# Where SyncE asks for the up weights, and where the flag's squares and product stand, in a two-layer gated network on one core

## The reference

```python
x = x + tanh(g_xattn[0]) * L0_xattn(ctx, layernorm(x))   # two graph attention layers, 8 heads of 32
x = x + tanh(g_ffn[0])   * L0_ffn(layernorm(x))          # silu(x gate^T * gs) * (x up^T * us), then down; inner 704
x = x + tanh(g_xattn[1]) * L1_xattn(ctx, layernorm(x))   # similarity of ctx, the top 76 of a row kept by sigmoid
x = x + tanh(g_ffn[1])   * L1_ffn(layernorm(x))          # 8 experts of width 512, the two best of a router
```

## Time and profile before

| | |
|---|---|
| median of 3 runs | 219.71 us (219.53 to 221.17) |
| the profiled execution's own time | 219.28 us |
| its span, first to last instruction | 217.3 us |
| outside the span | 1.98 us |
| granted TensorE clock over the span | 0.991 |
| PE busy | 201.7 us, 93% |
| DVE busy | 134.1 us, 62% |
| ACT and POOL busy | 85.8 and 85.9 us |

### The profile page before, as it was taken

One profiled execution on the slowest core, in us unless ns is written; L12 is line 12 of the kernel. 1 busy time (PEld: TensorE's weight loads), 2 busy tenths in 40 slices (PEclk: granted clock), 3 DMA queues, 4 the chain that ended last, 5 costly groups with the idle time before them and its releaser, 6 DMA issues.

```text
span 217.3 us, 3823 instructions
## 1 busy us (share of the span) xinstructions
PE 201.7 (93%) x1282; PEld 158.3 (73%) x1282; DVE 134.1 (62%) x461; ACT 85.8 (39%) x188; POOL 85.9 (40%) x107
## 2 busy tenths in 40 slices
PE   8999989999999999998989999999999999999930
PEld 7787764435885446788979998999973589999920
DVE  3696997999979969997788395853317601111200
ACT  2778653998001555034352263222225322222100
POOL 8256218420011020054640343543877656443222
PEclk9999999999999999999999999999999999999996
DMA  5768327139999115617142222322332310022322
GB/s 157 201 235 258 82 76 230 48 109 402 417 420 382 54 64 201 275 50 237 43 156 84 27 26 24 51 40 44 66 72 26 74 10 7 9 24 29 42 24 24
DMA packets 16797, 26.07 MB, mean 120 GB/s; under 512 B 4096, under 2 KB 12423, under 8 KB 16776
## 3 DMA queue, kind: packets, MB, share of 16 engines
q1 hardware_dynamic: 11328, 20.14, 25.8%
q0 software_dynamic: 4064, 5.25, 13.7%
q10 hardware_dynamic: 1382, 0.41, 1.1%
HBM read 21.34 MB, written 5.51 MB: 124 GB/s over the span
## 4 chain that ended last, share of the span: by engine, by line
PE 34%; DVE 32%; DMA 13%; issue 9%; ACT 7%; POOL 2%; DVEq 1%; POOLq 0%; ACTq 0%
PE PS L2081 13%; DMA out_dram<-a,ids_late 9%; PE PS L2113 6%; DMA out_dram<-zb,sidx 4%; PE PS L1784 3%; PE PS L2124 3%; DVE stat L1070 3%; DVE hT L1462 3%; ACT a L841 2%; PE PS L1848 2%; DVE work L1148 2%; DVE x L1322 1%; DVE mv L1077 1%; DVE work L1134 1%; DVE top L1144 1%
## 5 line engine op out<-in xcount | busy, mean ns | idle before, releaser
L2081 PE MATMUL PS<-hT,e 128*128 128x128 f32 x512 | 62.0, 276 | 1.1 <-ACT hT L970 1.1
L2081 PEld LDWEIGHTS PS<-hT,e 128*128 128x128 f32 x512 | 60.1, 192 | 2.9 <-ACT hT L970 1.9
L1966 PE MATMUL PS<-xnT,e 128*128 128x512 f32 x88 | 39.6, 598 | 2.0 <-DVE hT L1462 1.1
L1966 PEld LDWEIGHTS PS<-xnT,e 128*128 128x128 f32 x88 | 16.1, 190 | 22.2 <-issue 17.4
L1718 DVE TENSOR_TENSOR hT<-th,PS 128x512 f32<-128x512 f32 x15 | 10.3, 687 | 35.3 <-PE PS L2081 35.1
L2113 PE MATMUL PS<-e,hT 128*128 128x256 f32 x128 | 30.6, 382 | 0.2 <-DVE x L1500 0.2
L2113 PEld LDWEIGHTS PS<-e,hT 128*128 128x128 f32 x128 | 23.1, 190 | 2.8 <-issue 0.3
L646 POOL TENSOR_TENSOR rstd<-veps,nhalf 128x2 f32<-128x2 f32 x12 | 8.7, 728 | 39.4 <-DVE veps L1079 39.3
L709 POOL DMA_INDIRECT out_dram<-a,ids_early x8 | 13.0, 1629 | 24.1 <-ACT a L1004 11.4
L1980 PE MATMUL PS<-e,hT 128*128 128x256 f32 x96 | 21.7, 383 | 0.0
L1980 PEld LDWEIGHTS PS<-e,hT 128*128 128x128 f32 x96 | 17.9, 190 | 2.9 <-issue 0.5
(11 more groups left out here) (301 smaller groups left out, 316.5 us busy)
## 6 DMA issues: line engine op xcount, KB each, us to landing
e<-e_in SPq DMA_DIRECT2D x24, 512.0 KB, 8.6
x<-x_in SPq DMA_DIRECT2D x2, 512.0 KB, 6.3
graph_rows<-e SPq DMA_DIRECT2D x4, 256.0 KB, 2.1
out_dram<-x SPq DMA_DIRECT2D x4, 256.0 KB, 2.5
xn_rows<-xn SPq DMA_DIRECT2D x4, 256.0 KB, 2.4
e<-gw_in SPq DMA_DIRECT2D x1, 768.0 KB
e<-uw_in SPq DMA_DIRECT2D x1, 640.0 KB
e<-dw_in SPq DMA_DIRECT2D x1, 640.0 KB
```

The lines of the kernel that those rows point to most:

```text
L1966: mm = pe.matmul(PS[:, bank, :], w[:, k, it * P:(it + 1) * P], xnT[:, h, k, :], start=(k == 0), stop=(k == 1))
L2081: mm = pe.matmul(PS[:, bank + q, f * P:(f + 1) * P], w[:, k * F + f * P:k * F + (f + 1) * P], xgT[x_at][:, k, :], start=(k == 0), stop=(k ...
```

## The change

Three edits. SP waits for `row_picked[1]`, the gathered rows of tile 1, before it asks for `uw`, `gs`, `us`, `b1` and `ctxT`. On PE the flag's product goes ahead of `queries`. On ACT the second half of `sum_x` goes ahead of `weights`. No instruction is added or taken away besides SP's wait; line numbers behind it grow by one.

```diff
         PE_ORDER = [...
-                    ... ("weights", 0), ("feat", 1, 0), ("queries", 0), ("flag", 0),
+                    ... ("weights", 0), ("feat", 1, 0), ("flag", 0), ("queries", 0),
                     ("feat", 1, 1), ("sims", 0), ("sims", 1), ("graph_check", 0), ...
         ACT_ORDER = [...
-                     ("mix", 0), ("choice", 0), ("sum_hidden", 0), ("weights", 0), ("sum_x", 1), ("sum_hidden", 1),
+                     ("mix", 0), ("choice", 0), ("sum_hidden", 0), ("sum_x", 1), ("weights", 0), ("sum_hidden", 1),
                      ("feat", 1, 0), ("queries", 0), ("feat", 1, 1), ...
             for b in range(B):
                 if b == 2:
+                    sp.wait_ge(row_picked[1], 16)
                     load_up(uw, uw_in)
                     for v, src in ((gs, gs_in), (us, us_in)):
                         sp.dma_start(v[:, :], src).then_inc(ffn_loaded, 16)
                     load_general()
                 sp.wait_ge(token_ready, b + 1)
```

More of the change, by code:

```diff
@@ L413, in build @@
         PE_ORDER = [("hidden", 0), ("stay_warm", 7, 3), ("hidden", 1), ("feat", 0, 0), ("feat", 0, 1), ("hot", 0), ("mix", 0),
-                    ("stay_warm", 4, 3), ("choice", 0), ("stay_warm", 2, 3), ("compose", 0), ("weights", 0), ("feat", 1, 0), ("queries", 0), ("flag", 0),
+                    ("stay_warm", 4, 3), ("choice", 0), ("stay_warm", 2, 3), ("compose", 0), ("weights", 0), ("feat", 1, 0), ("flag", 0), ("queries", 0),
                     ("feat", 1, 1), ("sims", 0), ("sims", 1), ("graph_check", 0), ("hot", 1), ("stay_warm", 6, 6), ("choice", 1),
```

## The result

| | before | after |
|---|---|---|
| median of 20 runs each | 219.82 us | 220.69 us |
| ratio | | 1.0035, 95% interval 1.0018 to 1.0051 |
| profiled execution, its span | 219.28, 217.3 us | 220.44, 218.4 us |

The change makes the kernel slower by 0.35%, some 0.8 us (0.4 to 1.1 by the interval). It is small, but it lies clear of no change. I had forecast 0.2 us faster.

What follows compares the result with a forecast made beforehand. It took the flag's chain of waits as the early bound, then two nearly equal chains, DVE's and PE's. Of the flag's 0.83 us, 0.2 would remain: 219.71 - 0.2 = 219.5 us (219.2 to 219.7), measured range 218.8 to 220.6.

Steps and rivals of the forecast that it cites:

- ACT and the lead test: With `sum_x` early, DVE's lead test no longer waits for ACT's squares and ends at 19.26 us in place of 19.84.
- PE's start of the flag's product: Product at 19.31 us in place of 20.14; DVE's sums 0.83 us earlier, PE's own chain 0.17 us later.
- SP's wait, what it gives: Gathers 0 and 1 no longer share with uw; both had landed by 22.3 us anyway, so it gives nothing.
- SP's wait, what it takes: Gathers 2 and 3 now run beside uw: 0.5 us later each, at most some 1 us, no stall of DVE.
- Rival B: The fourth gather is late; landing at 26.0 us makes the kernel slower, 220.0 us; chance 0.08.
- Two nearly equal chains: Behind 30.5 us, DVE's search and PE's products: 32 matmuls take 14.29 us without a gap, PE then waits 0.27 us.
- compose as the first bound: DVE's `gix` waits for `compose`, which ends at 28.38 us; DVE goes on at 28.42, keeping 0.52 us of 0.83.
- The silu as a bound: At block 5, ACT's silu ends at about 51.98 us and holds DVE, which keeps 0.2 us of its 0.5.
- The loads' lateness, rival C: uw, gs or us reach PE late, at the far end 32.2 us, costing 1.5 us: 221.2 us; chance 0.05.

Runs made afterwards that it cites:

- e2: The kernel after without SP's wait, so the PE and ACT orders alone; ratio to the kernel before 0.9994 (0.9976 to 1.0012).
- e4: The kernel after with SP waiting for the fourth gathered tile (`row_picked[3]`) in place of the second; ratio to the kernel before 0.9985 (0.9963 to 1.0007).
- e7: The kernel after with uw in two loads of 320 KB, one ahead of SP's wait and one behind; 220.23 us in one run.
- e8: The kernel after with uw, gs, us at their old place, only the general path's loads behind SP's wait; ratio to the kernel before 0.9986 (0.9965 to 1.0007).
- e10: The kernel before with only PE's order changed, the flag's product ahead of `queries`; ratio to the kernel before 1.0016 (0.9998 to 1.0035).
- e12: The kernel after with SP waiting for the third gathered tile (`row_picked[2]`) in place of the second; ratio to the kernel before 0.9982 (0.9960 to 1.0003).
- e5: The kernel after without SP's wait, `lead_ready` waited for last, second half's `gix` behind its first feature pair; ratio to the kernel before 0.9988 (0.9966 to 1.0009).
- e6: e5 plus the queries in two halves with the flag's product between them; ratio to the kernel before 1.0005 (0.9987 to 1.0024).
- e9: e6 plus SP's wait, placed at the fourth gathered tile; ratio to the kernel before 0.9973 (0.9956 to 0.9990).
- e1: The kernel before with SP's wait for the second gathered tile alone, both orders unchanged; ratio to the kernel before 1.0021 (0.9999 to 1.0042).
- e3: The kernel after without SP's wait, queries in two halves with the flag's product between them; ratio to the kernel before 0.9986 (0.9964 to 1.0008).
- e11: The kernel before with only ACT's order changed, `sum_x` ahead of `weights`; ratio to the kernel before 1.0002 (0.9981 to 1.0022).

## Why the prediction was wrong

*ACT and the lead test*: right. `sum_x` at 16.4, the test free of ACT's squares, ended 0.40 us earlier than before (19.29 + 0.15 against 19.84 in the earlier trace rows), by the common clock 0.50; I had 0.58. The missing 0.08 is one small step of the test that took 0.24 us in place of 0.17 (`sum_hidden`'s end, by my own terms, was 19.00 and not 19.05; nothing hangs on it).

*PE's start of the flag's product*: mis-sized. I let 0.05 us pass between the end of the test and the product, as much as the profile of before shows from the end of ACT's L855 (25.99 + 1.09 = 27.08) to PE's L1866 (27.13); it took 19.70 - 19.44 = 0.26, and 0.26 again in e2, e4, e7, e8, e10 and e12. `token_ready` stands behind `lead_ready` in PE's waits; with `lead_ready` last, e5 took 0.15, so a wait written behind the late one cost 0.11 though it had long been met. With the 0.08 of the test and 0.05 in the product and the queries, PE's chain is 0.52 us late (4.03 against 3.51), not 0.17, and DVE 0.57 earlier at its first add, not 0.83.

*SP's wait, what it gives*: wrong. "both had landed by 22.3 even beside uw" came from a count of packets: 97 had passed by 22.25, and I read them as those of gathers 0 and 1. They need not have been: e2 and e5 show tile 1 landing 4.75 and 4.82 us from its issue. My estimate from them for the profile of before is 18.77 + 4.8, about 23.6, a quarter of a microsecond ahead of DVE's add at 23.82, where no wait shows it. Without uw beside it tile 1 lands within 21.68 - 18.87 = 2.81 us (SP's wait in the kernel after). So uw did hold a gather, and the edit's aim was sound; but there was little to win. With the wait at the third or fourth gather, e12 and e4 are at -0.19 and -0.24 us, where the orders alone, with uw at its old place, are at -0.19.

*SP's wait, what it takes*: **the step that failed.** "so I take 0.5 for each, and no stall": the delay of the fourth gather was 1.8 us, from a landing 3.0 us after its issue to one 4.8 us after, and so beyond my upper bound of 1 us too. It makes the whole loss: on the axis of before it landed at 26.31 - 0.10 = 26.21, and DVE had wanted it at 25.36 + 0.40 = 25.76, which is 0.45 us late; block 5 is 0.47 late, PE's end 0.44. Rival B was this mechanism at this place, with its point of decision near: landing from 25.6 on makes it slower, it landed at 26.3. I gave it 0.08, since I took the average pace of two pairs for the delay of one gather. My upper bound of 1 us, the time of the 95 packets once more, was nearer but took it that gathers and load move side by side, and here they did not: from 24 to 25 us uw had 158 packets and the gather none, and from 23 to 24 the gather had none while the loads took 49.2% of the engines. Why it stood there, and whether it had packets to hand over in that time, no row shows; that stays open.

*Two nearly equal chains*: wrong. I took 14.29 us for 32 matmuls as "without a gap". The gap is in the row of weight loads, which I had not read. PE's weight loads of before near 38 us:

```profile
37.66 0.30 PEld L1966 LDWEIGHTS PS<-xnT,e 128*128 128x128 f32 x2 [0.88 <-DVE hT L1462]
38.20 0.19 PEld L1966 LDWEIGHTS PS<-xnT,e 128*128 128x128 f32 x1 [0.24 <-issue]
```

The row of matmuls merges over that wait for DVE, whose cost is 0.31 us: the matmuls start at 37.02, 37.67 and 38.20, elsewhere 0.43 apart. So PE had more to spare ahead of 45 us, 0.66 us and not 0.27: in e2 it is 0.49 late at 13.90 and 0.17 early at its 33rd matmul (27.80 against 27.97). In these kernels DVE carries the end, and PE's idle time costs only by way of `compose`, which holds `gix`.

*compose as the first bound*: right in kind. e12 shows it:

```profile
28.94 0.16 DVE L1313 TENSOR_SCALAR gix<-PS 128x4 uint32<-128x4 f32 x1 [0.32 <-PE PS L1877]
```

DVE is 0.57 us early at its first add and 0.16 early at its second-half features; in e4 0.38 and 0.21. *The silu as a bound*: not seen at 0.41 us (e6).

*The loads' lateness, rival C*: did not come. uw landed 4.3 us from its issue, at 26.0, and us, the last of the three, 4.9 us from 22.60, at 27.5; PE wanted them at 31.

*The remainder.* The two profiled spans differ by 1.1 us: 0.10 is the start, 0.44 the change, and 0.56 the additions behind PE's last product, where the profile of before has the shortest stretch of all fourteen, those of kernels without SP's wait among them; that execution (219.28) was as fast as the fastest of the 20 runs (219.27). The granted clock is no rival: its mean is 0.987 over the kernel after's runs, and 0.986 to 0.987 over those of before that stand beside the experiments. The medians differ by 0.4 to 1.1 us; whether anything besides the 0.44 us is in them stays open.

## What to carry to other kernels

A load that is asked for behind a wait does not leave the traffic: here uw, no longer beside the second gather, met the fourth, which landed 4.8 us from its issue in place of 3.0 and was wanted 0.45 us before it came. So ask what comes next and how soon it is wanted, and place the wait late in a group of short transfers, if the load's reader has time for it: with SP's wait at the third or the fourth gather the fourth landed at 3.0 us (e12, e4), and `ffn_up` waited for no load. And first ask what the wait can win: here the well-placed one gained at most 0.05 us over none. Before two chains are called equal, read the waits of the weight loads too: here a merged row of matmuls hid one that cost 0.31 us. And a count of one queue's packets does not say whose they are: 97 had passed by 22.25 us, and tile 1 landed, by my estimate, at 23.6.

## What the runs showed that I had not expected

An indirect gather of 128 KB lands 2.9 to 3.0 us from its issue alone (e4, e9), and 4.8 us where a 640 KB load is asked for 0.2 us behind it (the kernel after, e1) or some 3 us ahead (e2, e5). With the load 1.5 us behind it (e12) it is 3.0. With the loads at their old place, the fourth gather varied between executions, from 2.9 us in e6 over 3.8 in e10 to 3.9 us in e5.

The third small step of the flag took 0.30 to 0.42 us in five kernels and 0.17 in the other nine, and in all five it stands at about one place beside POOL's issue. In e9, the third small step of the flag and the gather that POOL was issuing; then the same pair in e3:

```profile
21.32 0.41 DVE L1250 TENSOR_SCALAR sums<-sums 128x2 f32<-128x2 f32 x1
...
20.75 1.00 POOL L669 DMA_INDIRECT e<-graph_rows,gix  x1 [0.41 <-issue]
```

```profile
20.95 0.30 DVE L1249 TENSOR_SCALAR sums<-sums 128x2 f32<-128x2 f32 x1
...
20.27 1.01 POOL L668 DMA_INDIRECT e<-graph_rows,gix  x1 [0.30 <-issue]
```

The same step took 0.17 us in the kernel before, at 21.18, when that gather's issue (at 20.09) was over. In e4, e8 and e9 it starts 0.56 to 0.57 us behind the start of POOL's issue, in e3 and e6 0.68 us behind; in all five it ends 0.97 to 0.98 us behind it. In the kernel after, e2, e7 and e12 it starts 0.52 to 0.53 us behind, is done by 0.70, and takes 0.17. One-hot steps (`hot_rows`) are longer there too beside the fourth gather: one that starts 0.54 to 0.57 us behind takes 0.53 to 0.56 us in place of 0.35 and ends at 1.10 in the kernel before, e1, e3, e4, e8, e9 and e11, but costs nothing there: the first add starts 1.78 us behind the flag's write with such a step between them (before, 21.64 to 23.42) and without (the kernel after, 21.17 to 22.95). So in e4, e8 and e9 the earlier flag lost up to 0.25 us of what it had won, which is where they have their later first add, and e3 and e6 lost half of that. Not every step at this place is longer: in e12 a one-hot step 0.54 us behind takes 0.35, in e10 one 0.73 behind the third gather's issue takes 0.36, and in e5 the flag's fourth step, 0.62 behind, its usual 0.22. No run here takes POOL's issue away, so that the issue holds the step is my guess and not shown.
